# Cross attention with paired key heads and a context that arrives already transposed

## What is computed

```
x = x + linear_attention(layernorm(x))            # 16 heads of 16, elu+1 features
x = x + cross_attention(layernorm(x), ctx)        # 16 query heads, 4 key/value heads
x = x + moe(layernorm(x))                         # 8 experts, top 2, and a shared expert
```

```
Q = (query @ Wq).reshape(b, q_len, G, Hpg, dh)    # G = 4 groups, Hpg = 4 heads in each
K = (ctx @ Wk).reshape(b, kv_len, G, dh)          # dh = 16, so K has 64 channels
V = (ctx @ Wv).reshape(b, kv_len, G, dh)
scores = einsum('bqghd,bkgd->bghqk', Q / sqrt(dh), K) + alibi, masked
out = einsum('bghqk,bkgd->bqghd', softmax(scores), V) @ Wo
```

## Time and profile before

| | |
|---|---|
| three runs | 481.43, 484.37, 485.26 us; median 484.37 us |
| span of the profiled execution | 481.2 us (481.18) |
| mean granted clock of TensorE | 0.931 of full speed |
| busy TensorE matmul / weight load | 81% / 68% |
| busy VectorE / ScalarE / GpSimd | 62% / 48% / 45% |
| attention stage | up to about 275 us |

### The profile page before, as it was taken

How to read it: one execution, slowest core, us unless ns; L and a number is a source line. 1 busy time by engine, 2 the same in 40 slices (tenths; PEclk the granted TensorE clock), 3 DMA queues, 4 the chain that set the end, 5 groups by cost and what they waited for, 6 DMA issues and landing times.

```text
span 481.2 us, 12458 instructions
## 1 busy us (share of the span) xinstructions
PE 389.4 (81%) x4000; PEld 326.6 (68%) x4000; DVE 298.3 (62%) x809; ACT 230.6 (48%) x576; POOL 215.6 (45%) x252
## 2 busy tenths in 40 slices
PE   6787889888898898998987878199999999999400
PEld 4466667666676676776866668189998888889300
DVE  1455777778777777778653297146765665556265
ACT  1233466544665446644653476057635555555200
POOL 1134376665766657665463004735403334343300
PEclk9698999999999989989999989679999999999755
DMA  8720105141041510500000001211213333333286
GB/s 243 198 97 12 53 5 143 54 140 58 5 137 53 140 53 0 140 11 12 12 2 1 2 0 49 105 67 66 81 51 101 111 118 108 106 111 111 75 283 220
DMA packets 30422, 40.13 MB, mean 83 GB/s; under 512 B 6322, under 2 KB 23602, under 8 KB 30386
## 3 DMA queue, kind: packets, MB, share of 16 engines
q1 hardware_dynamic: 24626, 28.09, 20.4%
q0 software_dynamic: 3456, 9.46, 5.5%
q10 hardware_dynamic: 2304, 2.10, 1.3%
HBM read 22.82 MB, written 16.81 MB: 82 GB/s over the span
## 4 chain that ended last, share of the span: by engine, by line
PE 57%; DVE 17%; issue 12%; DMA 5%; ACT 3%; another core or an unknown queue 2%; POOL 2%; DVEq 1%; POOLq 0%; ACTq 0%; SPq 0%
PE ps L749 17%; PE ps L523 6%; PE ps L640 4%; PE ps L587 3%; PE ps L627 3%; DMA yg<-y_rows 3%; DVE sc L1227 3%; PE ps L530 3%; PE ps L602 3%; PE ps L568 2%; DMA y_rows<-e_y,out_row 2%; PE ps L593 2%; DVE xn L1221 2%; PE ps L679 2%
## 5 line engine op out<-in xcount | busy, mean ns | idle before, releaser
L497 POOL DMA_INDIRECT y_rows<-e_y,out_row x40 | 38.5, 962 | 69.7 <-ACT e_y L1093 33.6
L749 PE MATMUL ps<-w_hi,xh 128*128 (+1 forms) x144 | 50.8, 353 | 17.0 <-DVE xl L1346 14.3
L438 POOL TENSOR_TENSOR sc<-sc,smax 128x1024 f32<-128x1024 f32 x16 | 31.7, 1984 | 43.4 <-DVE smax L1233 43.4
L489 POOL DMA_INDIRECT xs_rows<-x_send,pos x32 | 31.0, 969 | 40.3 <-DVE pos L1445 19.7
L749 PE MATMUL ps<-w_hi,xl 128*128 (+1 forms) x144 | 47.8, 332 | 0.0
L749 PE MATMUL ps<-w_lo,xh 128*128 (+1 forms) x144 | 47.5, 330 | 0.0
L749 PEld LDWEIGHTS ps<-w_hi,xh 128*128 128x128 f32 x144 | 27.8, 193 | 21.5 <-issue 14.2
L431 POOL TENSOR_TENSOR bias_t<-alibi,key_off 128x1024 f32<-128x1024 f32 x16 | 37.9, 2368 | 0.0
L404 POOL TENSOR_TENSOR st<-mv,eps 128x1 f32<-128x1 f32 x32 | 6.1, 192 | 65.7 <-DVE mv L1147 33.8
L523 PE MATMUL ps<-wkv,xn1T 128*128 128x512 f32 x64 | 32.8, 638 | 0.5 <-ACT xn1T L929 0.5
L1221 DVE TENSOR_SCALAR xn<-x_all,mv,rs 128x256 f32<-128x256 f32 (+1 forms) x16 | 28.6, 1789 | 2.1 <-POOL rs L406 1.9
(11 more groups left out here) (179 smaller groups left out, 1178.0 us busy)
## 6 DMA issues: line engine op xcount, KB each, us to landing
w_stage<-in_w_ffn_dram SPq DMA_DIRECT2D x12, 496.0 KB, 3.9
xs_rows<-zeros SPq DMA_DIRECT2D x5, 1028.0 KB, 7.7
xs<-xs_rows SPq DMA_DIRECT2D x40, 128.5 KB
yg<-y_rows SPq DMA_DIRECT2D x16, 256.0 KB, 3.9
ctx_sb<-in_ctx_dram SPq DMA_DIRECT2D x16, 128.0 KB, 2.0
out_dram<-y ACTq DMA_DIRECT2D x16, 128.0 KB, 4.0
x_all<-in_x_dram SPq DMA_DIRECT2D x1, 1792.0 KB, 10.3
y_rows<-e_y,out_row POOLq DMA_INDIRECT x40
```

The source lines that it names most:

```text
L438: nc.gpsimd.tensor_tensor(v, v, spread(smax[:, :].rearrange("p (h o) -> p h o", o=1), 2, S), ALU.subtract).then_inc(sm["sub_ready"], 1)
L489: nc.gpsimd.indirect_dma_start(out=xs_d[:, :], out_offset=bass.IndirectOffsetOnAxis(ap=pos[:, t, r:r + 1], axis=0), in_=x_send[:, t, r, :] ...
L497: nc.gpsimd.indirect_dma_start(out=y_d[:, :], out_offset=bass.IndirectOffsetOnAxis(ap=out_row[:, q:q + 1], axis=0), in_=e_y[:, q, :], in_o ...
L749: mm = T.matmul(out_ap, lhs, rhs[rows, cols], start=st, stop=en)
```

## The change

The host reorders the query heads, and with them the columns of `xwq`, the rows of `xwo` and the order of the alibi slopes. Now each block of 128 query channels has, in every 32 channels, two heads that belong to two neighbouring groups, and the same four groups appear in both blocks. One block of 128 key channels (the 64 key channels twice) serves both: `xwk` is loaded in that form, `xwk_rep` and its copy on VectorE are gone, `project_ctx` has two written matmuls for the keys, `k_bd` is half as large. The values are split the same way: `v_block` copies 64 elements of each partition where it copied 128.

The host also gives the context with channels on partitions. It is loaded into `ctxT`, which has two buffers; the load of tile `t` waits for `project_ctx` of tile `t - 2`, not for the transpose of tile `t - 1`. The two context transposes are gone, `copy_xn2T` copies 256 columns, `project_ctx` waits for the load and no longer for ScalarE, and `transpose_x` and `project_q2` have a new wait on `xn2T_ready`.

```diff
-            xwk = sb_attn("xwk", [P, KC, GROUPS * DH])
-            xwk_rep = sb_attn("xwk_rep", [P, KC, GROUPS, HEADS // GROUPS, DH])
+            xwk = sb_attn("xwk", [P, KC, 2 * GROUPS * DH])
...
-            def next_ctx(t):
-                sp.wait_ge(sm["xcT_mm"], t)
-                sp.dma_start(ctx_sb[:, :], ctx_d[bass.ds(t * P, P), :]).then_inc(sm["ctx_in"], 16)
+            def next_ctx(t, q):
+                wait(sp, sm["ckv_mm"], t - 1)
+                sp.dma_start(ctxT[:, q, :, :], ctx_d[:, bass.ds(t, 1), :, :].rearrange("p o k t -> p (o k) t")
+                             ).then_inc(sm[f"ctx_in{q}"], 16)
...
                 pe.wait_ge(sm["ln1_done"], t + 1)
+                wait(pe, sm["xn2T_ready"], t - 1)
                 for k in range(KC):
                     mm = T.transpose(ps[:, A0, k * P:(k + 1) * P], xn1[:, k * P:(k + 1) * P], ident[:, :])
...
-            def transpose_xc(t):
-                pe.wait_ge(sm["ctx_in"], 16 * (t + 1))
+            def transpose_x2(t):
                 pe.wait_ge(sm["q1_ready"], 2 * (t + 2 if has(t, 1) else t + 1))
-                for k in range(KC):
-                    T.transpose(ps[:, A0, (KC + k) * P:(KC + k + 1) * P], ctx_sb[:, k * P:(k + 1) * P], ident[:, :])
                 pe.wait_ge(sm["ln2_done"], t + 1)
...
-                pe.wait_ge(sm["xcT_ready"], t + 1)
+                pe.wait_ge(sm[f"ctx_in{q}"], 8 * (t - q) + 16)
                 wait(pe, sm["sc_ready"], t)
-                for c in range(2):
-                    for k in range(KC):
-                        T.matmul(ps[:, B2, c * P:(c + 1) * P],
-                                 xwk_rep[:, k, 2 * c:2 * c + 2, :, :].rearrange("p g h d -> p (g h d)"),
-                                 xcT[:, KC + k, :], start=(k == 0), stop=(k == KC - 1))
+                for k in range(KC):
+                    T.matmul(ps[:, B2, 0:P], xwk[:, k, :], ctxT[:, q, k, :], start=(k == 0), stop=(k == KC - 1))
...
-                A.activation(xcT[:, :, :].rearrange("p c t -> p (c t)"), ps[:, A0, :], ACT.Copy).then_inc(sm["xcT_ready"], 1)
+                A.activation(xn2T[:, :, :].rearrange("p c t -> p (c t)"), ps[:, A0, 0:D], ACT.Copy).then_inc(sm["xn2T_ready"], 1)
...
-                    last = A.activation(k_bd[:, :, h, :], ps[:, B2, 0:D].rearrange("p (c t) -> p c t", c=2), ACT.Copy,
+                    last = A.activation(k_bd[:, h, :], ps[:, B2, 0:P], ACT.Copy,
                                         scale=row_head[:, h:h + 1])
...
-                    last = A.activation(v_bd[:, q, :, h, 0:DH], vv, ACT.Copy, scale=row_half[:, h:h + 1])
+                    last = A.activation(v_bd[:, q, :, h, 0:DH], vv[:, :, h, :], ACT.Copy, scale=row_half[:, h:h + 1])
...
-                V.tensor_copy(xwk_rep[:, :, :, :, :].rearrange("p k g h d -> p (k g) h d"),
-                              spread(xwk[:, :, :].rearrange("p k (g o d) -> p (k g) o d", g=GROUPS, o=1), 2, HEADS // GROUPS)
-                              ).then_inc(sm["consts_v"], 1)
```

More of the change, by code:

```diff
@@ L212, in build @@
             xn2 = sb_attn("xn2", [P, D])
-            xcT = sb_attn("xcT", [P, 2 * KC, P])
+            xn2T = sb_attn("xn2T", [P, KC, P])
             q2T = sb_attn("q2T", [P, KC, P])
-            k_bd = sb_attn("k_bd", [P, 2, 2, P])
-            v_bd = sb_attn("v_bd", [P, 2, SEQS * GROUPS, 2, DH + 1])
+            k_bd = sb_attn("k_bd", [P, 2, P])
+            v_bd = sb_attn("v_bd", [P, 2, SEQS * GROUPS // 2, 2, DH + 1])
             smax = sb_attn("smax", [P, HEADS])
@@ L268, in build @@
             attn_mm xbo_ready x1_ready
-            ln2_st ln2_mv ln2_ve ln2_rs ln2_done xcT_mm xcT_ready ckv_mm q2_mm kbd_ready vbd_ready q2T_ready
+            ln2_st ln2_mv ln2_ve ln2_rs ln2_done xn2T_mm xn2T_ready ckv_mm q2_mm kbd_ready vbd_ready q2T_ready
             scores_mm bias_ready sc_ready smax_ready sub_ready exp_ready rsum_ready o2_ready o2T_mm
@@ L598, in project_q2 @@
             def project_q2(t):
+                pe.wait_ge(sm["xn2T_ready"], t + 1)
                 wait(pe, sm["xn3T_ready"], t - 2)
@@ L601, in project_q2 @@
                     for k in range(KC):
-                        mm = T.matmul(ps[:, B3, c * P:(c + 1) * P], xwq[:, k, c * P:(c + 1) * P], xcT[:, k, :],
+                        mm = T.matmul(ps[:, B3, c * P:(c + 1) * P], xwq[:, k, c * P:(c + 1) * P], xn2T[:, k, :],
                                       start=(k == 0), stop=(k == KC - 1))
@@ L726, in body @@
                 if has(t, 0):
-                    transpose_xc(t)
+                    transpose_x2(t)
                 if has(t, -2):
@@ L1553 @@
     slopes = (2.0 ** (-8.0 / HEADS * np.arange(1, HEADS + 1))).astype(np.float32)
-    order = [c * 8 + j * 2 + h for j in range(4) for c in range(2) for h in range(2)]
+    head = lambda c, j, h: GROUPS * (2 * (j % 2) + h) + 2 * c + j // 2
+    order = [head(c, j, h) for j in range(4) for c in range(2) for h in range(2)]
+    q_cols = [(GROUPS * g + 2 * c + r) * DH + d for c in range(2) for r in range(2) for g in range(GROUPS) for d in range(DH)]
+    o_rows = [head(c, j, h) * DH + e for c in range(2) for j in range(4) for h in range(2) for e in range(DH)]
     rel = (np.arange(S)[None, :] - (pos % S)[:, None]).astype(np.float32)
@@ L1565 @@
     arrays = {
-        "x": i["x"], "ctx": i["ctx_2048"], "mask": i["mask_BxS2_bf1"].view(np.uint8),
+        "x": i["x"], "ctxT": np.ascontiguousarray(i["ctx_2048"].reshape(TILES, P, KC, P).transpose(3, 0, 2, 1)),
+        "mask": i["mask_BxS2_bf1"].view(np.uint8),
         "ident": np.eye(P, dtype=np.float32),
```

56 lines of the change are left out of this document (28 added, 28 removed).

## The result

Both kernels were timed in turn on the same chip, 15 runs each: the changed kernel takes 486.81 us in the median (483.04 to 489.43), the one before 484.37 us (480.79 to 486.94). The ratio is 1.0061, with a 95% interval of 1.0035 to 1.0087: 0.35 to 0.87% slower, where 0.4% less was forecast and 486.0 us was the upper end of the range.

What follows compares the result with a forecast made beforehand. The steady loop was taken to be bound by `xn1`, TensorE from L516, `split_low` with `xn2`, and `score_add`. Terms -0.5 and -1.0 (iterations 1, 2), -0.2 (low clock), -0.15 (iteration 16) sum to -1.85: 482.5 us, range 479.0 to 486.0.

Steps and rivals of the forecast that it cites:

- Low stretches later: Later steady iterations: stretches at 1.2 for 2.4 GHz on TensorE, in perhaps five of 12 iterations; together -0.2 us.
- Rival (B): From L663 to L555: low clock pays the saving back, 1.2 us per fully covered iteration; eight give 491.2 us; chance 0.06.
- Key projection: TensorE, each tile: two of four matmuls go, but L516 waits for `xn1` anyway; 0 us, other bound -5.3.
- Rival (A): Steady iterations: TensorE's work is the bound, each gets shorter by 0.445 us; 477.2 us; chance 0.12.
- Context transposes: TensorE, ahead of its wait for `xn2`: 0.43 us per tile goes, that wait only becomes longer; 0 us.
- The loop, with `split_low` and `xn2` in it: Steady loop: `xn1`, TensorE from L516, `split_low` with `xn2` (2.26 us), `score_add`, maximum; nothing the change removes lies on it.
- Iterations 1 and 2: Start: key projection no longer waits for the copy and is halved; -0.5 us in iteration 1, -1.0 in iteration 2.
- ScalarE, loads, new waits: Shorter ScalarE copies hidden behind TensorE's queue in steady state, loads issued early, new waits already met; 0 us each.
- The -0.15 of iteration 16: ScalarE's exponential in iteration 16 can start at most 0.15 us earlier, after `subtract_max`; all counted, -0.15 us.

Runs made afterwards that it cites:

- e0: The changed kernel as it is, run again on another chip: 471.53 us against 467.08 for the kernel before, ratio 1.0079.
- e1: Changed kernel with the two context transposes put back at their old place, results unread: 463.90 us, ratio 0.9912 to the kernel before.
- e6: Changed kernel with one unread matmul of zeros (256 columns, 0.70 us) where the context transposes stood: 477.57 us against 484.85 for the kernel before, ratio 0.9872.
- e3: Changed kernel with both the unread context transposes and four key matmuls put back: ratio 1.0037 to the kernel before.
- e2: Changed kernel with four key matmuls again (second pair unread), without the context transposes: ratio 1.0111 to the kernel before.
- e5: Kernel before with only `split_low` moved behind the next tile's `rstd1` on GpSimd: 457.95 us, ratio 0.9458 to the kernel before.
- e4: Changed kernel with `split_low` moved behind the next tile's `rstd1` on GpSimd: 456.97 us, ratio 0.944 to the kernel before.

## Why the prediction was wrong

**The step that failed** is the term "Low stretches later", -0.2 us with bounds of -1.1 and +1.5. It was a count times a price. I expected the clock to fall in "perhaps five of 12" iterations; it fell nine times (ten in e0). I put three more at 0.3 us each. The low stretches of the eleven periods cost 168.09 - 162.90 = 5.2 us, 0.65 for each of eight. The two before had cost 15.53 - 14.98 = 0.55 and 15.62 - 14.99 = 0.63, 1.2 us, much as I had assumed. The term therefore measures +4.0 us, not -0.2, and lies beyond its upper bound of +1.5. The mechanism was in the prediction, that 0.43 us less in the piece before the clock fell would bring more falls, and e1 and e6 confirm it, but the size was carried over from two cheap stretches. A price that depends on where the stretch falls in the iteration can't be taken from two samples that both fell early, and the count was a guess without a row. Rival (B) had the mechanism, the place and the price of the dear case right (1.2 us, measured 16.04 against about 14.8), and its count (eight) nearly; but of nine stretches only three were fully covered, so 491.2 us was too much. I had given it 0.06. The Trainium skill (TensorE: Matmul & The Clock Gate, A second HAM failure mode), which I had cited for (B), points the right way with its frequent short idles that make the clock swing. This trace agrees with it in this: between 50 and 225 us the clock fell from 2.4 to 1.2 GHz nine times, although TensorE's matmuls were busy for 128.42 of the 150 us from 60 to 210.

**Key projection, 0.** Right about its place, a little too strict in size. In an undisturbed iteration 0.11 to 0.18 us went (14.98 to 14.87 and 14.80), not 0.445. Over 11 periods that is 165.66 - 1.2 - 162.90 = 1.6 us, which I had at 0 with -5.3 as the other bound. Rival (A), a period near 14.5, fell. In e1, where the clock holds, the wait of the weight load for `xn1` grew to 0.43 us on average in six iterations and to 0.5 in the five others, which the view puts down to nothing that it shows, where 0.6 was forecast:

```profile
PEld ps L517 <- DVE xn L1151: 2.6, 6, 0.5
PEld ps L517 <- issue: 2.5, 5, 0.6
```

**Context transposes, 0.** Wrong in the way that matters. "What hides them is `xn2`; without them that wait becomes longer and nothing else is late" is true of the timeline: the wait of the `xn2` transposes grew from 0.63 to 1.10 us, as forecast. But they had a use that no wait shows. e1 puts just them back and takes 1.7% off the changed kernel's ratio (0.9912 for 1.0079), e6's zeros in their place 1.9% (0.9872 for 1.0061). With four key matmuls they are worth less, 0.7% (e3 for e2).

**The loop, with `split_low` and `xn2` in it.** Right: `xn2` still takes 2.26 us beside `split_low`, and e5 takes 5.4% off the kernel before by moving `split_low` alone; the same move takes the changed kernel from 1.006 to 0.944. The engine with the highest share, TensorE, was not the one to relieve.

**Iterations 1 and 2, -1.5 together.** The two first traces show -4.8 us to the 2nd `score_add`, more than forecast, but that is mostly chance. The trace of before stands alone with 56.74 (its clock was low from 11.5 to 14.9 us and from 18.4 to 25.2), and in all other traces, e3 with all of before's TensorE work and e5 among them, the 2nd `score_add` stands between 51.6 and 53.9. Like for like (e4 against e5) it is 51.98 against 52.45, -0.5 us. The term was three times too large.

**ScalarE, loads, new waits.** Nothing late was found for the terms at 0. The key copies take 0.62 us, inside the 0.41 to 0.83 that stood as bounds. The -0.15 of iteration 16 came true: the period from the 15th to the 16th `score_add` is 10.84 us for 10.97. That `xn2T_ready`, the load and the shorter copies cost nothing is what the waits say; e3's 0.37% over the kernel before leaves room for something there that they do not show.

**The rest**: the routing is 1.07 us longer in the changed kernel's trace, with two low stretches in it (from 280 and 290 us) for one before (from 277.8). The sum by the measured terms is -0.5 at the start, -1.6 for the undisturbed periods, +4.0 for the low stretches and -0.1 for iteration 16, 1.8 us; with the routing, which stands on one trace of each, 2.9. The medians say +2.4. The +3.2 us up to the last scatter and the -0.8 behind it are left out, as stages that stand on one trace of each, so the nearness of the sums to 2.4 is in part luck.

What stays open: what sets the phase of the falls; what the 0.37% of e3 are; and why the stage from the positions to the last scatter takes 51 to 56 us where the kernel before takes 484 us and 40.6 where it takes 467. No experiment was made on the first or the last.

## What to carry to other kernels

Before work is taken out of TensorE's gaps because "something else hides it", look at the granted clock in the windows around that gap: if the clock already falls there now and then, the hidden work may be what holds it up, and taking it away can cost more than the work on the path that goes with it. If it must go, put a matmul of zeros into the same gap and time both. Better still, close the gap: find the operation that makes TensorE wait and see what runs beside it on the other engines.

## What the runs showed that I had not expected

- A matmul of zeros, 0.70 us in an iteration of 14.8 us and read by nobody, makes the changed kernel 1.3% faster than the one before, and no low stretch is left in the steady part of its trace; one of 0.49 us makes it 0.5% faster. Real data isn't needed for it.
- In the traces of the two kernels, the same low stretch of some 3.4 us costs 0.1 to 0.6 us if it begins ahead of `score_add`, and 1.1 to 1.3 us if it begins 1.1 to 1.4 us behind its start.
- The idle time before a fall is short: the longest single wait in the window ahead of the fall at 174.4 is 1.10 us, with TensorE's matmuls busy for 1.82 of 3.50 us.
- A `tensor_scalar` of 128x256 on VectorE takes 0.41 us alone and 2.26 us beside GpSimd's 2.29 us `split_low`; moving that one GpSimd instruction was worth nine times the change that was studied (5.4% for 0.6%), with the opposite sign.
- The trace of e2, with four key matmuls, has six low stretches and that of e0, with two, has ten, although these matmuls stand behind the gap.
